# Block-local attention of a decoder layer: queries stationary on 32-column tiles in place of keys stationary, softmax in chunks of four groups

## What is computed

```python
nb = 22; CHUNK = 12; CTX = 24; P = 25                  # windows of 12 queries
q_blocked = pad(q).reshape(B, nb, CHUNK, H, D)          # B, H, D = 4, 8, 16
k_ctx, v_ctx = _extract_block_context(k), ...(v)        # 24 keys per window, 12 of them past
matrix_ac = einsum('bnchd,bnkhd->bhnck', q_blocked, k_ctx)
matrix_bd = _rel_shift(einsum('bnchd,phd->bhncp', q_blocked, rel_k))   # 25 positions
logits = tanh((matrix_ac + matrix_bd) / 50) * 50
out = einsum('bhnck,bnkhd->bnchd', softmax(logits), v_ctx)
x = x + out[:, :S].reshape(B, S, H * D) @ Wpost.T
```

## Time and profile before

| | us |
|---|---|
| median of 3 runs | 530.58 (529.27 to 530.89) |
| the profiled execution | 525.21 |
| its span, first to last instruction | 522.9 |
| mean granted clock of TensorE | 0.934 |

### The profile page before, as it was taken

One profiled execution on the slowest core, in us unless ns is written; L12 is line 12 of the kernel. 1 busy time (PEld: TensorE's weight loads), 2 busy tenths in 40 slices (PEclk: granted clock), 3 DMA queues, 4 the chain that ended last, 5 costly groups with the idle time before them and its releaser, 6 DMA issues.

```text
span 522.9 us, 8263 instructions
## 1 busy us (share of the span) xinstructions
PE 476.5 (91%) x3150; PEld 353.4 (68%) x3150; DVE 322.1 (62%) x697; ACT 183.2 (35%) x276; POOL 238.0 (46%) x208
## 2 busy tenths in 40 slices
PE   1969997779879999999999999967999999999997
PEld 0559996557546767666776667646777777888885
DVE  7642537399998765776557976663355443265554
ACT  4640141444435553554345554221323632300000
POOL 5232024097976777677776876703223233000000
PEclk9975568799989999999999999968999999999999
DMA  4086500000000000000000002010222221000000
GB/s 130 0 186 130 143 3 2 1 1 2 1 0 1 2 1 0 2 1 1 0 1 3 1 2 85 0 41 21 60 61 60 61 64 38 1 6 10 6 10 11
DMA packets 29676, 15.06 MB, mean 29 GB/s; under 512 B 11745, under 2 KB 27334, under 8 KB 29638
## 3 DMA queue, kind: packets, MB, share of 16 engines
q1 hardware_dynamic: 28936, 14.25, 10.6%
q10 hardware_dynamic: 702, 0.28, 0.2%
HBM read 12.56 MB, written 1.97 MB: 28 GB/s over the span
## 4 chain that ended last, share of the span: by engine, by line
PE 74%; DVE 16%; POOL 4%; issue 3%; ACT 3%; DVEq 0%; POOLq 0%; ACTq 0%
PE psum L793 9%; PE psum L958 8%; PE psum L941 8%; PE psum L813 5%; PE psum L1091 4%; PE psum L1128 4%; PE psum L1127 4%; PE psum L1129 4%; PE psum L1093 4%; PE psum L1092 4%; PE psum L977 3%; PE psum L876 2%; PE psum L994 2%; PE psum L968 2%; DVE rden L1344 2%
## 5 line engine op out<-in xcount | busy, mean ns | idle before, releaser
L448 POOL TENSOR_TENSOR e_part<-e_sb 128x512 f32<-128x512 f32 x64 | 91.0, 1439 | 37.5 <-DVE e_sb L1337 37.5
L651 ACT ACTIVATE e_sb<-psum 128x1024 f32<-128x1024 f32 x64 | 62.3, 1023 | 17.2 <-PE psum L941 17.2
L941 PE MATMUL psum<-q_t,kT 64*128 64x256 f32 x512 | 64.3, 389 | 0.0
L958 PE MATMUL psum<-e_sb,v_sb 128*64 128x256 f32 x512 | 63.5, 391 | 0.0
L473 POOL TENSOR_TENSOR xeT_lo<-xeT,xeT_hi 128x512 fp32r<-128x512 f32 x24 | 30.9, 1290 | 66.9 <-ACT xeT_hi L665 66.9
L440 POOL TENSOR_TENSOR k_rot<-rope_a,rope_b 128x512 f32<-128x512 f32 x32 | 42.0, 1312 | 40.2 <-DVE rope_b L1232 40.2
L1344 DVE RECIPROCAL rden<-psum 128x256 f32<-128x256 f32 x32 | 56.0, 1749 | 2.1 <-PE psum L968 2.0
L1516 DVE SCALAR_TENSOR_TENSOR x_sb<-psum,dw,x_sb 128x128 f32<-128x128 f32 x96 | 33.7, 351 | 34.7 <-PE psum L1129 32.1
L941 PEld LDWEIGHTS psum<-q_t,kT 64*128 64x128 f32 x512 | 47.0, 186 | 10.5 <-issue 5.6
L626 ACT ACTIVATE kT<-psum 128x512 f32<-128x512 f32 x32 | 19.1, 598 | 97.2 <-PE psum L876 97.0
L1337 DVE TENSOR_SCALAR e_sb<-e_sb 128x1024 f32<-128x1024 f32 x64 | 48.1, 788 | 7.9 <-ACT e_sb L651 7.9
(11 more groups left out here) (183 smaller groups left out, 846.5 us busy)
## 6 DMA issues: line engine op xcount, KB each, us to landing
w_raw<-in_L_ffn_W_dram SPq DMA_DIRECT2D x24, 256.0 KB, 2.7
ctx_sb<-in_ctx_dram SPq DMA_DIRECT2D x4, 256.0 KB, 4.7
raw<-in_L_xattn_Wkv_dram SPq DMA_DIRECT2D x4, 256.0 KB, 4.7
bd_dram<-bd_raw SPq DMA_DIRECT2D x2, 412.5 KB
bd<-bd_dram SPq DMA_DIRECT2D x1, 792.0 KB, 6.1
vbd<-v_dram SPq DMA_DIRECT2D x8, 73.3 KB
vbd<-v_dram SPq DMA_DIRECT2D x8, 71.7 KB
v_dram<-v_tok SPq DMA_DIRECT2D x4, 136.0 KB, 3.3
```

The costliest lines, as they stand in the source:

```text
L448: pool.tensor_tensor(e_part[:, p % 2, half, :, :], e_sb[:, i % ERING, :, 0, :], e_sb[:, i % ERING, :, 1, :], ALU.add)\
L651: act.activation(e_sb[:, i % ERING, :, :, :].rearrange("p a k t -> p (a k t)"), psum[:, a:a + 2, :].rearrange("p a b -> p (a b)"), ACT.Exp ...
L941: mm = pe.matmul(psum[:, 2 * (i % 2) + a, t * S:(t + 1) * S], kT[rows, p % 3, kt * P:(kt + 1) * P], q_t[rows, j % 2, p % 2, :], start=True ...
L958: mm = pe.matmul(psum[DX * a:DX * a + DX, pv_bank(p), 0:S], v_sb[g % 2][:, kt, 2 * pp + a, :], e_sb[:, i % ERING, a, t, :], start=(kt == 0 ...
```

## The change

Windows are no longer counted per batch: there are 88 (WALL), in 22 groups of four (NGRP), in six chunks of four groups (NCH, the last has two). qM holds each window's 24 query columns side by side. A window's queries, taken as 32 columns, become the stationary operand on one of four 32-column tiles of PE, and the keys (96 columns) or the positions (100) move. Logits so come with queries on partitions; they are softmaxed in place per chunk, turned back by PE (`turn_weights_local`), copied to prT by ACT, and then used as before. `turn_outputs` uses transposes, and ACT's `outputs_turned` drops the padding.

bd_raw is stored by four DMAs of ACT and read back by eight of SP. The units are not woven into the logits any more; they follow them. On SP, everything of the window copies stands ahead of the third raw weight block; on ACT, `weight_hi(4)` and `weight_hi(5)` stand behind the last chunk. DVE clears the second part of vbd later, and the context statistics move between the chunks. POOL's order of `weight_rest`, `key_sum` and `rstd_of` is as it was, with three memsets placed elsewhere.

```diff
+    WALL = B * NB
+    NGRP = WALL // WG
+    CG = 4
+    NCH = -(-NGRP // CG)
+    QW = 2 * CH
+    REL = NPOS * G
+    SPLIT_SLOT = NBP * B // 2 + CG
...
+                ns = (slice(0, SPLIT_SLOT), slice(SPLIT_SLOT, NW))[pair]
...
+                    sp.wait_ge(s["v_padded"], 32)
+                    sp.wait_ge(s["v_stored"], 16 * B)
+                    sp.wait_ge(s["v_zeroed"], 3)
+                    spread_values(0)
+                    sp.wait_ge(s["bd_stored"], 16 * WG)
+                    sp.wait_ge(s["consts"], 6)
+                    for i in range(WG):
+                        shifted = bd_dram[i:WALL:WG].rearrange("k (h c) r -> h k (c r)", h=2)
+                        for half in range(2):
+                            sp.dma_start(bd[QT * i + CH * half:QT * i + CH * (half + 1), :, :],
+                                         shifted[half, :, 0:CH * GK].rearrange("k (c r) -> c k r", r=GK)).then_inc(s["shifted"], 16)
+                    spread_values(1)
+                if n >= 2:
+                    sp.wait_ge(s["w_lo_done"], n - 1)
+                src = x_wkv[:, c * GC:(c + 1) * GC] if c < 4 else x_wq[:, (c - 4) * GC:(c - 3) * GC]
+                sp.dma_start(raw[:, n % 2, :], src).then_inc(s[f"ld_raw{n % 2}"], 16)
+                if n == 1:
                     sp.dma_start(cos_sb[:, :, :], rope_cos.rearrange("(t p) d -> p t d", p=P)).then_inc(s["ld_rope"], 16)
                     sp.dma_start(sin_sb[:, :, 1, :], rope_sin.rearrange("(t p) d -> p t d", p=P)).then_inc(s["ld_rope"], 16)
+                    sp.wait_ge(s["pad_set"], 2)
...
+            pool.memset(bd[:, :, :], 0.0).then_inc(s["consts"], 1)
...
+            pool.wait_ge(s["added_done"], 1)
+            pitch = CG * P + CH
+            pool.memset(prT[:, 0:(NCH - 1) * pitch].rearrange("p (c q) -> p c q", q=pitch)[:, :, CG * P:pitch], 1.0).then_inc(s["consts"], 1)
+            end = NGRP * P + (NCH - 1) * CH
+            pool.memset(prT[:, end:end + CH], 1.0).then_inc(s["consts"], 1)
             for n in range(4, 6):
                 weight_rest(n)
...
+            def positions_out(c):
+                act.wait_ge(s["bd_ps"], c + 1)
+                ks = groups(c)
+                act.activation(bd_raw[:, ks.start:ks.stop, :].rearrange("p k r -> p (k r)"), psum[:, REL_BANK[c], 0:len(ks) * REL], ACT.Copy)\
+                   .then_inc(s["bd_raw_done"], 1)
+            for c in range(2):
+                positions_out(c)
             for j in range(2):
                 act.wait_ge(s["v_tok_ps"], j + 1)
                 act.activation(v_tok[:, 4 * j:4 * j + 4, :, 0:DA].rearrange("p t h d -> p (t h) d"),
                                bank(2 * j).rearrange("p (n d) -> p n d", d=DA), ACT.Copy).then_inc(s["v_tok_done"], 1)
...
+            for c in range(2, NCH):
+                positions_out(c)
+            act.wait_ge(s["bd_raw_done"], NCH)
+            for i in range(WG):
+                act.dma_start(bd_dram[i:WALL:WG].rearrange("k q r -> q k r"), bd_raw[QT * i:QT * i + QW, :, :]).then_inc(s["bd_stored"], 16)
+            for n in range(2):
+                weight_hi(n)
...
+                act.wait_ge(s["added_done"], c + 1)
+                ks = groups(c)
+                at = lg[:, ks.start:ks.stop, :].rearrange("p k r -> p (k r)")
                 act.activation(at, at, ACT.Tanh, scale=1.0 / CAP).then_inc(s["capped_done"], 1)
-                act.wait_ge(s["capped_done"], b + 1)
-                act.activation(pr[:, b, :, 0:S], at, ACT.Exp, scale=CAP).then_inc(s["prob_done"], 1)
+                act.wait_ge(s["capped_done"], c + 1)
+                act.activation(at, at, ACT.Exp, scale=CAP).then_inc(s["prob_done"], 1)
+            def weights_turned(c):
+                act.wait_ge(s["pT_ps"], c + 1)
+                ks = groups(c)
+                act.activation(prT[:, ks.start * P + c * CH:ks.stop * P + c * CH], psum[0:GK, LOGIT_BANK[c], 0:len(ks) * P], ACT.Copy).then_inc(s["pT_done"], 1)
+            def outputs_turned(c):
+                act.wait_ge(s["oT_ps"], c + 1)
+                ks = groups(c)
+                act.activation(oT[:, ks.start * WG * CH:ks.stop * WG * CH].rearrange("p (w t) -> p w t", t=CH),
+                               psum[:, TURN_BANK[c], 0:len(ks) * P].rearrange("p (w t) -> p w t", t=QT)[:, :, 0:CH], ACT.Copy)\
+                   .then_inc(s["oT_done"], 1)
...
+            for m in range(KC, UNITS):
+                value_unit(m)
+            local_softmax(0)
+            local_softmax(1)
+            weights_turned(0)
+            local_softmax(2)
+            weights_turned(1)
+            local_softmax(3)
+            weights_turned(2)
+            outputs_turned(0)
+            local_softmax(4)
+            weights_turned(3)
+            outputs_turned(1)
+            local_softmax(5)
+            weights_turned(4)
+            outputs_turned(2)
+            weights_turned(5)
+            outputs_turned(3)
+            outputs_turned(4)
+            outputs_turned(5)
+            weight_hi(4)
+            weight_hi(5)
...
-            for w, at, ps in ((0, 7, "q_ps"), (1, 5, "k_ps")):
-                for j in range(2):
-                    pe.wait_ge(s["xT_done"], j + 1)
+            for j in range(2):
+                pe.wait_ge(s["xT_done"], j + 1)
+                for w, at, ps in ((1, 5, "k_ps"), (0, 7, "q_ps")):
                     pe.matmul(bank(at - j), awT[:, w, :], xT[:, 2 * j:2 * j + 2, :], start=True, stop=True).then_inc(s[ps], 1)
...
+                for k in groups(c):
+                    at = (k - CG * c) * REL
+                    for i in range(WG):
+                        w = WG * k + i
+                        mm = pe.matmul(psum[QT * i:QT * i + QT, REL_BANK[c], at:at + REL], qM[:, QW * w:QW * w + QT],
+                                       relM[:, :, :].rearrange("p n g -> p (n g)"), start=True, stop=True)
+                mm.then_inc(s["bd_ps"], 1)
...
+                for k in groups(c):
+                    at = (k - CG * c) * GK
+                    for i in range(WG):
+                        b, n = divmod(WG * k + i, NB)
+                        w = WG * k + i
+                        mm = pe.matmul(psum[QT * i:QT * i + QT, LOGIT_BANK[c], at:at + GK], qM[:, QW * w:QW * w + QT],
+                                       kM[:, b, CH * n:CH * n + CTX, :].rearrange("p t g -> p (t g)"), start=True, stop=True)
+                mm.then_inc(s["logit_ps"], 1)
+            def turn_weights_local(c):
+                pe.wait_ge(s["prob_done"], c + 1)
+                for k in groups(c):
+                    at = (k - CG * c) * P
+                    mm = pe.transpose(psum[0:GK, LOGIT_BANK[c], at:at + P], lg[:, k, :], ident[:, :])
+                mm.then_inc(s["pT_ps"], 1)
...
+            def turn_outputs(c):
+                pe.wait_ge(s["oq_done"], c + 1)
+                if c < 4:
+                    pe.wait_ge(s["pT_done"], c + 3)
+                else:
+                    pe.wait_ge(s["oT_done"], c - 1)
+                for k in groups(c):
+                    at = (k - CG * c) * P
+                    mm = pe.transpose(psum[:, TURN_BANK[c], at:at + P], o_q[:, c % 2, k - CG * c, :], ident[:, :])
+                mm.then_inc(s["oT_ps"], 1)
...
+            for c in range(2):
+                relative(c)
...
+            for c in range(2, NCH):
+                relative(c)
+            for c in range(NCH):
+                local_logits(c)
+            turn_context(0, 6, "ct_ps")
+            for m in range(UNITS):
+                unit(m)
+            turn_weights_local(0)
+            turn_weights_local(1)
             local_values(0)
+            turn_weights_local(2)
             local_values(1)
             turn_outputs(0)
+            turn_weights_local(3)
             local_values(2)
+            turn_outputs(1)
             local_project(0)
-            turn_outputs(1)
+            turn_weights_local(4)
             local_values(3)
+            turn_outputs(2)
             local_project(1)
-            turn_outputs(2)
-            pe.wait_ge(s["x1_done"], 2 * TPB)
+            turn_weights_local(5)
+            local_values(4)
+            turn_outputs(3)
+            local_values(5)
+            turn_outputs(4)
+            turn_outputs(5)
+            local_project(2)
+            local_project(3)
             turn_keys(0)
-            local_project(2)
-            turn_outputs(3)
-            turn_latents(0, 1, "lat_ps")
+            turn_latents(0, 5, "lat_ps")
             queries(0)
-            local_project(3)
             turn_keys(1)
             turn_keys(2)
...
-            for i in range(2):
-                dve.memset(vbd[:, i * NW // 3:(i + 1) * NW // 3, :, :, :], 0.0).then_inc(s["v_zeroed"], 1)
-                first_statistics(i)
+            dve.memset(vbd[:, 0:NW // 3, :, :, :], 0.0).then_inc(s["v_zeroed"], 1)
+            first_statistics(0)
+            first_statistics(1)
...
```

(44 more changed lines are left out.)

253 lines of the change are left out of this document (78 added, 175 removed).

## The result

The changed kernel takes 533.16 us (median of 8 runs, 529.05 to 535.20), the kernel before, run beside it, 528.27 us (median of 8, 525.13 to 530.89). The ratio is 1.0075, with a 95% interval of 1.0038 to 1.0111: **0.75% slower, about 4 us**. A second comparison gave 1.0074 (1.0043 to 1.0104). The profiled execution took 531.83 us with a span of 530.1; before, the span was 522.9.

What follows compares the result with a forecast made beforehand. It took PE (74% of the chain) as the bound, its relief lost to SP's queue, ladder and chunk loop: rstd at 90.8 plus 12.1 puts scores(0) 3.3 us later, rounded to 3.0 on 530.6: 533.6 us, range 528.0 to 541.

Steps and rivals of the forecast that it cites:

- Front: Start of the kernel up to v stored: about 1.6 us won by moving DVE's second vbd memset; v stored at 26.4.
- Window copies: SP's vbd loads: two groups of eight at 0.82 us issue each, 6.5 us a group, plus 0.5 us of stall.
- Landing: Third raw weight block: issued at 44.7, landed 4.7 us later, at 49.4.
- Ladder: Weight chain through ACT, POOL, DVE and four units on PE: from 49.4 to the last value copy at 61.3.
- Chunk loop: Chunks after the units: 8 us to the first outputs (69.3), then four cycles of 3.3 us, to 82.5.
- Tail: weight_hi(4), rests and rstd: from 82.5 to 90.8, then 12.1 us to scores(0) at 102.9.
- New matmuls: Logits and relative matmuls on PE: 0.026 us a record, 4.5 us for 176 logits records, 4.7 us for 176 relative ones.
- that rival: New matmuls do not overlap on the tiles: 0.145 us a record, v_tok 7.6 us later, 541 us; chance 0.03.
- Carried to the end one for one: From scores(0) on no instruction changes, so any shift there reaches the end unchanged.
- the hole (21.4 us): Sign of being right: PE idle over 15 us after unit 3, from about 37 to 55.
- the faster SP: All 24 loads issued at 0.53 us, raw block landed 5.6 us earlier: 528.0; chance 0.22, shared with a shorter chunk cycle.
- The second: PE stays at 1.2 GHz through the chunks, a cycle some 5.2 us, four add 7.6: 541; chance 0.16.

Runs made afterwards that it cites:

- e1: Changed kernel with the third and fourth raw weight blocks issued on SP ahead of the bd loads and second window copies; 520.82 us, ratio 0.9853 to the kernel before.
- e2: Changed kernel with the latents' rstd moved on POOL ahead of the Wq remainders and two contexts; 525.87 us, ratio 0.9945 to the kernel before.
- e3: Changed kernel with both the edits of e1 and e2; 514.36 us, ratio 0.9742 to the kernel before.
- e10: Changed kernel with e2's order, weight blocks 0 and 1 rounded early on ACT, raw blocks 2 and 3 loaded before v's stores, context loads moved; 509.78 us, ratio 0.9647.
- c1: Changed kernel run again with nothing edited, for a second profile; 532.64 us, ratio 1.0074 to the kernel before.
- e7: Changed kernel with DVE's second memset of vbd put back at the front; 537.39 us, ratio 1.0179 to the kernel before.
- e8: Changed kernel with SP waiting for ACT's four stores to land before the first eight window copies; one run, 533.90 us.
- e4: Changed kernel with 14 additional 512-column matmuls on PE in its second hole, behind the first turn of keys; 531.28 us, ratio 1.0042 to the kernel before.
- e6: Changed kernel with four local logits matmuls in a row on one column tile instead of a new tile each time; one run, 533.49 us.
- e5: Changed kernel with each of the 88 local logits matmuls issued twice; one run, 536.02 us.
- e9: Changed kernel with 44 additional 256-column matmuls on PE in its first hole, between units 3 and 4; 532.01 us, ratio 1.0058 to the kernel before.

## Why the prediction was right, and where it was luck

I gave 533.6 us, 3.0 more than before; 533.16 was measured, by the ratio 4 more, and `scores(0)` stood where I had put it (102.93 for 102.9). The mechanism is shown: e1, e2, e3 and e10 take back 11.7, 6.8, 17.5 and 22.6 us by moving loads, POOL's order and, in e10, ACT's rounding of two blocks, with the same matmuls. But the exact hit is a sum of errors that cancel, and luck of the execution besides: in c1, the same kernel, `scores(0)` came at 105.66. Term by term, in the first profile:

- *Front.* The window copies began at 24.71, not 26.4: -1.7. Half is `v_tok`, which ended at 21.55 for my 22.4 (the moved memset alone is worth 3.5 us or more by e7), half the landing of the last store, 2.4 us for 3.3. My own terms (22.4, 1.0, 3.3) add to 26.7, not 26.4.
- *Window copies.* The step that failed most. I took 0.82 from the first row and only 0.5 us of stall; both groups went at 1.16, 18.4 us for 13.5: +4.9. The row with 9.40 was the nearer one, since stores ran beside it, as here. e8 shows that 0.82 holds for copies alone. I had quoted the rule of the Trainium skill (DMA: Bandwidth & Descriptors, "Why a DMA increments its semaphore by 16 and not by 1") by which these loads use 12 engines, had read them as near the limit of these, and then priced them as if nothing shared them. The DMA share, from which I said that the trace agrees, does not bear that out: in e8, with 12-partition loads alone in flight, it stood at 1.05 to 1.09 from 42 to 50, above 12/16. bd took 4.4 for 4.8: -0.4. Gaps between the groups: +0.2.
- *Landing.* The fourth block bound the ladder, not the third. It landed 6.1 us after the third was issued, for my 4.7: +1.4.
- *Ladder.* From there 10.1 us to the last value copy for my 11.9: -1.8. One remainder (1.26) was done while the fourth block was still landing, and the units took 4.7 for 5.5.
- *Chunk loop.* 17.4 us to the last copies for 21.2: -3.8. Half is the start (6.2 for 8; with a dip it is 7.6). I had counted six passes of ACT; there are eight, but the six with the other terms that I named (0.5, 0.6, 0.08, 0.63) add to 6.2, not 8. The other half is the short last chunk of two groups, that I charged as a full one: the cycles were 2.6, 3.3, 3.1 and 1.6, for 3.3 each.
- *Tail.* POOL's part 8.4 us for 8.3. From `rstd` to `scores(0)` 13.2 for 12.1: +1.1. I had taken 0.8 off for the projection that stood there before, and nothing came of it: the turn of keys now waits for ACT's q_t instead, and from the first query matmul to that turn go 2.43 us in both kernels. The other 0.4 is the clock: 1.01 us from the second turn of keys to `scores(0)`, at 0.50, for 0.56. e4 shows that it is not to be had by filling the hole.
- *New matmuls.* 176 logits records in 4.0 us for 4.5, relative ones in 4.2 for 4.7; e6 shows that the price rests on the change of tile. Without it a record costs 0.046 us, not the 0.145 at which I had priced that rival. e5 doubled them in the hole.

The rows of PE on which the tail's reading rests, before, and then after:

```profile
94.72 0.58 PE L890 MATMUL psum<-lat_hi,wq_hi 128*128 128x256 f32 x1 [2.26 <-DVE lat_lo L1318]
...
97.15 1.09 PE L876 MATMUL psum<-ident,k_rot 128*128 128x128 f32 x4
99.02 0.63 PE L876 MATMUL psum<-ident,k_rot 128*128 128x128 f32 x4 [0.78 <-ACT kT L626]
```

```profile
97.62 0.58 PE L957 MATMUL psum<-lat_hi,wq_hi 128*128 128x256 f32 x1 [2.33 <-DVE lat_lo L1385]
...
100.05 1.09 PE L943 MATMUL psum<-ident,k_rot 128*128 128x128 f32 x4 [0.78 <-ACT q_t L688]
101.92 1.09 PE L943 MATMUL psum<-ident,k_rot 128*128 128x128 f32 x4 [0.78 <-ACT kT L678]
```

The terms add to 0.0 us; in c1 the same sum is +2.8. "Carried to the end one for one" did not hold: +3.35 at `scores(0)` is +4.3 at the first exponent and 7.2 in the spans, and from `scores(0)` to the end of the execution go 425.6 us in the profile before and 426.4 to 429.6 in those of the changed kernel and its edits. The two profiled executions differ by 6.6 us, the medians by 4.9, the ratio by 4. The kernel before has executions near 525 (clock 0.934) and near 530 us (0.922), and its one profile is of the first kind, while I put the 3.0 on a median of the second. Where `scores(0)` stands in the second, no trace shows.

Of my signs, the hole (21.4 us) and ACT idle on the third block came; that block landed at 52.1 for 47 to 52, `rstd` ended at 89.7 for 90.8, and the chunks were not 3 to 3.6 us apart. One sign of being wrong came too, the clock at 0.50 after 62 (from 86 on). It was a poor sign, since the kernel before has it there as well.

Of the rivals, the faster SP (528.0) fell by the raw block's landing at 52, with a landing before 46.4 as its condition; e1 confirms its reasoning, with the landing at 39.6 and a gain. (The shorter chunk cycle of 2.6 that I put beside it would give 2.8 us, not the same 5.6.) The second, PE at 1.2 GHz through the chunks, is partly true: the dip of 1.4 to 2.7 us at their start comes in c1 and in e1 to e6 and e9, not in the first profile, e7 and e8, and in c1 the clock is back from 71 on. The falls come, in c1 at 67.7 and in e9 at 65.1, where PE has had nothing but turns of weights and pauses since the units; in e2 one comes at 87.4, in a pause of 3.05 us behind a turn of keys. The Trainium skill (TensorE: Matmul & The Clock Gate, "Part 4: PE-mode transpose") says that transposes do not count as PE activity in the way that matmuls do. The falls in c1 and e9 fit that; but PE also stood idle between these turns, the first profile had the same turns and no fall there, and no run tells the one from the other.

## What to carry to other kernels

When matmuls on the critical engine get cheaper, ask first what will be late in their place: here a weight load that the new order had put behind 24 small copies, and an `rstd` that stood behind work nobody waited for. Moving both gave 2.6% over the kernel before (e3), and taking the weight loads out of the ladder altogether 3.5% (e10). Price a DMA's issue by a row with the same company in the queues, not by the cleanest row.

## What the runs showed of the hardware

- The issue of a window copy of 65 to 80 KB takes 0.76 to 0.91 us alone (eight in 6.52, e8). Beside four stores of 206 KB from ACT's queue single copies take up to 1.8 and eight take 8.84 to 10.84 (eleven profiles of the changed kernel and its edits); behind the eight bd loads the first four take up to 2.6, and then again 0.76. Not every transfer does this: in the kernel before, copies went at 0.76 from 34.5 on, while loads still landed at 302 GB/s (34 to 35).
- Matmuls of 96 columns on alternating 32-column tiles take 0.022 us a record, four in a row on one tile 0.046, at the full clock (e6, one run).
- Filling a hole with matmuls does not carry the clock through the sparse work behind it. In e4 the filling ended at 96.7 with the clock at 1.00, and it fell at 101.0, behind turns, pauses and the query matmuls. In e9 the clock had fallen to 0.50 by 34.5 and came back to 1.00 under the filling, at about 41; it fell again at 65.1, between two groups of turns. No gain in time is shown in either.
